# A recommendation tower on one core: turns moved one lookup sooner, table halves split by ScalarE's rounding, dots in uneven parts, last bias on TensorE

## The reference: what is computed

```python
e = jnp.stack([tbl_0[ids[:, 0]], ..., tbl_25[ids[:, 25]]], axis=1)   # (2048, 26, 128)
T = jnp.concatenate([dense[:, None, :], e], axis=1)                  # (2048, 27, 128)
Z = jnp.einsum('bnd,bmd->bnm', T, T)
iu0, iu1 = jnp.triu_indices(27, k=1)
z = Z[:, iu0, iu1]                                                   # (2048, 351)
h = jnp.concatenate([z, r_dense], axis=1)
h = jnp.maximum(h @ W_top1 + b_top1, 0.0)                            # 512 wide
h = jnp.maximum(h @ W_top2 + b_top2, 0.0)                            # 256 wide
y = h @ W_top3                                                       # (2048, 1)
```

## Time and profile before

| what | value |
|---|---|
| median of 3 runs | 508.34 us (504.71, 508.34, 509.56) |
| the profiled execution, its own time | 507.75 us |
| its span, first to last instruction | 505.9 us |
| mean granted clock of TensorE | 0.879 of full |
| busy: PE, weight load, DVE, ACT, POOL | 77%, 69%, 44%, 35%, 50% |

### The profile page before, as it was taken

How to read it: one execution, slowest core, us unless ns; L and a number is a source line. 1 busy time by engine, 2 the same in 40 slices (tenths; PEclk the granted TensorE clock), 3 DMA queues, 4 the chain that set the end, 5 groups by cost and what they waited for, 6 DMA issues and landing times.

```text
span 505.9 us, 9897 instructions
## 1 busy us (share of the span) xinstructions
PE 391.6 (77%) x4042; PEld 348.4 (69%) x4042; DVE 220.4 (44%) x786; ACT 174.9 (35%) x220; POOL 252.6 (50%) x263
## 2 busy tenths in 40 slices
PE   5841766695499858988599857988589866999997
PEld 3731656595398737978389745978379754988887
DVE  5521662584364404923346314734148223744322
ACT  4303540353225413343214422354114622244241
POOL 6776473647436554536544574456553575360000
PEclk9965796888689978988599987999699996999999
DMA  8961131125501322114311243113221151013221
GB/s 219 250 202 50 32 100 30 49 48 137 159 22 43 94 78 84 39 36 121 106 35 32 65 115 93 28 48 97 78 82 34 44 134 47 23 45 69 48 50 23
DMA packets 45878, 39.07 MB, mean 77 GB/s; under 512 B 32930, under 2 KB 39113, under 8 KB 45834
## 3 DMA queue, kind: packets, MB, share of 16 engines
q1 hardware_dynamic: 36014, 21.40, 16.0%
q0 software_dynamic: 8192, 16.79, 12.8%
q10 hardware_dynamic: 1628, 0.25, 0.3%
HBM read 32.40 MB, written 6.02 MB: 76 GB/s over the span
## 4 chain that ended last, share of the span: by engine, by line
PE 51%; another core or an unknown queue 28%; DVE 7%; issue 6%; ACT 6%; DMA 1%; DVEq 0%; SPq 0%; ACTq 0%
PE look_ps L756 25%; PE gram_ps L782 9%; PE mlp_ps L802 8%; DVE hot L467 5%; PE look_ps L766 5%; PE mlp_ps L812 3%; ACT T L618 2%; DVE gram L491 1%; ACT T L610 1%; ACT tab_hi L586 1%; PE look_ps L823 1%; PE look_ps L845 1%; DMA ids_all<-in_ids_dram 1%; DVE dense L480 0%
## 5 line engine op out<-in xcount | busy, mean ns | idle before, releaser
L421 POOL DMA_INDIRECT rows<-in_tbl_dram,ids_all x240 | 234.2, 976 | 196.6 <-PE look_ps L766 115.1
L467 DVE TENSOR_SCALAR hot<-ids_near 125x256 fp32r<-125x256 f16 x640 | 147.0, 301 | 151.0 <-remote 104.9
L756 PE MATMUL look_ps<-hot,tab_hi 125*128 125x256 f32 x616 | 162.4, 300 | 43.1 <-issue 32.5
L756 PE MATMUL look_ps<-hot,tab_lo 125*128 125x256 f32 x616 | 158.0, 293 | 5.7 <-issue 5.6
L756 PEld LDWEIGHTS look_ps<-hot,tab_hi 125*128 125x128 f32 x616 | 123.4, 200 | 47.7 <-issue 35.7
L756 PEld LDWEIGHTS look_ps<-hot,tab_lo 125*128 125x128 f32 x616 | 124.0, 201 | 6.1 <-issue 6.0
L618 ACT COPY T<-look_ps 128x384 f32<-128x384 f32 (+1 forms) x80 | 83.6, 1075 | 120.6 <-PE look_ps L766 108.1
L782 PE MATMUL gram_ps<-T 128*54 128x54 f32 x2048 | 72.9, 225 | 33.9 <-issue 27.1
L782 PEld LDWEIGHTS gram_ps<-T 128*54 128x54 f32 x2048 | 64.7, 140 | 45.1 <-issue 35.4
L610 ACT COPY T<-look_ps 128x512 f32<-128x512 f32 x32 | 38.6, 1206 | 108.0 <-PE look_ps L756 55.8
L491 DVE COPY gram<-gram_ps 128x432 f32<-128x432 f32 x64 | 38.0, 607 | 79.2 <-remote 53.4
(11 more groups left out here) (72 smaller groups left out, 146.0 us busy)
## 6 DMA issues: line engine op xcount, KB each, us to landing
dots<-gram SPq DMA_DIRECT2D x28, 182.2 KB
ids_near<-ids_rows SPq DMA_DIRECT2D x7, 640.0 KB
rows<-in_tbl_dram,ids_all POOLq DMA_INDIRECT x240
T<-in_tbl_dram SPq DMA_DIRECT2D x5, 448.0 KB
pairs<-dots SPq DMA_DIRECT2D x14, 117.0 KB
rows<-in_r_dense_dram SPq DMA_DIRECT2D x16, 64.0 KB
gram<-in_tbl_dram SPq DMA_DIRECT2D x2, 448.0 KB
pairs<-dots SPq DMA_DIRECT2D x7, 104.0 KB
```

The lines of the kernel that those rows point to most:

```text
L421: pool.indirect_dma_start(rows[:, t % 2, place[n], :], None, tables[n - 1], bass.IndirectOffsetOnAxis(ap=index[:, n - 1:n].bitcast(U32), a ...
L467: eq = nc.vector.tensor_scalar(hot[:VP, at % 2, c], ids_near[:VP, u % 2, k], float(c), None, ALU.is_equal)
L756: mm = pe.matmul(dst, w[:VP, k, c], hot[:VP, slot, c], start=(c == 0 and half == 0), stop=(c == CH - 1 and half == 1))
```

## The change

The change has six parts.

1. **Split of the tables.** `tab_hi` is now what ScalarE's write rounds the raw table to; `lead`, `top` and the semaphore `top_ready` are gone. ScalarE's copies for the first five tables stand ahead of the first look_out, those of the tables 1, 3 and 5 are moved from the loop to the start, and DVE subtracts in four instructions of 256 numbers in place of one of 1024 (`split`). Five raw buffers take the place of three, and the raw loads are issued sooner, ahead of the small weights.
2. **Turns.** In the first half of a unit u > 0, turn(u,1,2) stands ahead of look(u+1,1), turn(u,1,3) ahead of look(u+1,2), and turn(u,1,4) between the halves of layer1, on TensorE and on ScalarE alike. Unit 0 keeps its order.
3. **DVE in unit 0.** The splits of tables 1, 3 and 5 stand at other places, in one piece each.
4. **Dots.** The parts of a tile are 6, 8, 9 and 9 pieces, and 9, 9, 9 and 5 for the last tile.
5. **Last bias.** For the last tile the bias of the second layer is put into PSUM by one matmul (identity times bias) ahead of layer1, and DVE's addition after the last matmul is gone.
6. **Small weights** are issued on SP after load_dense(0, 1), ahead of the pair weights.

```diff
         def first_half(u):
             if u > 0:
-                return [("turn", u, 1, 0), ("turn", u, 1, 1), ("look", u + 1, 0), ("look", u + 1, 1),
-                        ("turn", u, 1, 2), ("look", u + 1, 2), ("turn", u, 1, 3), ("turn", u, 1, 4)]
+                return [("turn", u, 1, 0), ("turn", u, 1, 1), ("look", u + 1, 0), ("turn", u, 1, 2),
+                        ("look", u + 1, 1), ("turn", u, 1, 3), ("look", u + 1, 2), ("turn", u, 1, 4)]
...
+        def pieces(u, l):
+            ends = [9, 18, 27, NI] if u == END and l == 1 else [6, 14, 23, NI]
+            return list(zip([0] + ends, ends))
...
             def split(k):
-                lead(k)
-                rest(k)
+                dve.wait_ge(hi_ready, hi_count(k))
+                if k in WHOLE:
+                    dve.wait_ge(hot_looked, look_count(0, k))
+                for c in range(0, CH, 2):
+                    minus = nc.vector.tensor_tensor(tab_lo[:VP, k, c:c + 2], raw[k][:VP, c:c + 2],
+                                                    tab_hi[:VP, k, c:c + 2].bitcast(F32), ALU.subtract)
+                minus.then_inc(lo_ready, 1)
...
             def hi_out(k):
-                i = split_count(k) - 1
-                act.wait_ge(top_ready, i + 1)
-                nc.scalar.copy(tab_hi[:VP, k], top[2 if k in WHOLE else i % 2][:VP]).then_inc(hi_ready, 1)
+                act.wait_ge(raw_landed[k], 32)
+                nc.scalar.copy(tab_hi[:VP, k], raw[k][:VP]).then_inc(hi_ready, 1)
...
-            hi_out(0)
+            for k in LEADING[:5]:
+                hi_out(k)
             look_out(0, 0)
-            hi_out(2)
...
                 look(u + 1, 0)
+                turn(u, 1, 2)
+                look(u + 1, 1)
+                turn(u, 1, 3)
                 if u > 0:
-                    look(u + 1, 1)
-                    turn(u, 1, 2)
                     look(u + 1, 2)
                     layer1(u - 1, 0, 8)
-                    turn(u, 1, 3)
-                    layer1(u - 1, 8, 12)
                     turn(u, 1, 4)
-                    layer1(u - 1, 12, 16)
+                    layer1(u - 1, 8, 16)
...
+            pe.matmul(last_l2(1), ident[:], bias2[:], start=True, stop=False)
             last_layer1(1)
             last_layer2(1)
```

More of the change, by code:

```diff
@@ L17 @@
 MAX_ROUND = 4
-LOW_BITS = 12
 BLOCKS = 4
@@ L147, in dlrm_tower @@
         gram_flat = gram[:].rearrange("p s n q -> p (s n q)")
-        raw_slots = [table_at(spare, 0), table_at(spare, CH * D), table_at(gram_flat, 2 * CH * D)]
+        raw_slots = [table_at(spare, i * CH * D) for i in range(2)] + [table_at(gram_flat, i * CH * D) for i in range(3)]
         whole_raw = [table_at(w1[:].rearrange("p c f -> p (c f)"), 0), table_at(pairs[:].rearrange("p a c q -> p (a c q)"), 0),
@@ L303, in load_raw @@
             def load_raw(k):
-                if k not in WHOLE and in_turn.index(k) >= 3:
-                    sp.wait_ge(lo_ready, in_turn.index(k) - 2)
+                if k not in WHOLE and in_turn.index(k) >= len(raw_slots):
+                    sp.wait_ge(lo_ready, in_turn.index(k) - len(raw_slots) + 1)
                 src = tables[onehot[k]].rearrange("(p c) d -> p c d", c=CH)
@@ L362, in _ @@
             sp.dma_start(ids_all[:], ids_v).then_inc(ids_landed, 16)
-            for k in range(6):
+            for k in range(8):
                 load_raw(k)
             load_dense(0, 0)
-            load_raw(6)
-            load_small_weights()
-            load_raw(7)
+            load_raw(8)
             sp.wait_ge(ids_t_ready, UNITS)
@@ L484, in gram_out @@
                 if u == 0 and l == 0:
[L485 removed]
+                    dve.wait_ge(lo_ready, len(in_turn))
                 if u > 0 and l == 0:
                     dve.wait_ge(dots_stored, STORED * u)
[L488 removed]
+                for b, (first, end) in enumerate(pieces(u, l)):
                     dve.wait_ge(gram_done, BLOCKS * (2 * u + l) + b + 1)
[L490 to L493 removed]
+                    nc.vector.tensor_copy(gram[:, :, :, l * NI + first:l * NI + end],
+                                          gram_ps[:, b % 2, 0:2 * (end - first) * NV]
+                                          .rearrange("p (i s n) -> p s n i", s=2, n=NV)).then_inc(gram_free, 1)
             def y_out(u):
@@ L778, in products @@
                 src = T_tile(u, l).rearrange("p (g i s) n -> p g i (s n)", g=2, s=2)
-                for i in range(b * PER, (b + 1) * PER):
+                first, end = pieces(u, l)[b]
+                for i in range(first, end):
                     for g in range(2):
-                        at = (i - b * PER) * 2 * NV
+                        at = (i - first) * 2 * NV
                         mm = pe.matmul(gram_ps[64 * g:64 * g + 2 * NV, b % 2, at:at + 2 * NV], src[:, g, i],
@@ L845, in last_layer2 @@
                     mm = pe.matmul(last_l2(l), h1[:, c, l * P:(l + 1) * P], w2[:, c],
-                                   start=(c == 0), stop=(c == F1C - 1))
+                                   start=(c == 0 and l == 0), stop=(c == F1C - 1))
                 mm.then_inc(l2_done, 1)
```

93 lines of the change are left out of this document (29 added, 64 removed).

## The result

The changed kernel takes 532.51 us (median of 6 runs, 531.31 to 535.28) beside 508.33 for the kernel before: ratio 1.049, 95% interval 1.046 to 1.053. Timed once more (`after_again`) it took 532.06 beside 508.17, ratio 1.050 (1.045 to 1.054). The profiled execution has a span of 531.7 us.

A forecast was written before the change was run, and what follows sets the result against it. It took TensorE as busiest, but idling some 9 us a unit as its signals come late in long gather runs. 507.75 + 22.8 (turns) + 0.5 (split) = 531, given as 530; 8-in-10 range 491 to 538.

The forecast's parts named there:

- case A: Whole kernel: the long run of gathers in first halves makes TensorE's signals late; 530 us, 519 to 538; chance 0.56.
- the turns: First halves of units 1 to 6: earlier turns make a run of 8 gathers; 3.8 us more each, 22.8 in all.
- the split: Table split at the start: nothing gained up to 54.8 us, then split(9) waits for ScalarE's copy; +0.5 us, -1.8 to +1.1.
- The second half: Second halves of the units: order and run of 14 gathers stay, each moves as a whole; no cost.
- Uneven dots: Dots in uneven parts, each of 16 tiles: nothing, -0.2 to +0.2 us a tile.
- last bias: End of the kernel: DVE's 0.43 us addition goes, TensorE gains 0.45 us; zero, -0.5 to +0.5.
- Case B: First halves: turn 2 signals after GpSimd is free, so gathers run as 4 and 7; 495 us; chance 0.22.
- Case C: First halves: long runs do no harm, the dots gain 2.7 us in each of six; 492 us; chance 0.10.

The follow-up runs named there:

- turns_alone: The kernel before with only the new order of the turns in units 1 to 6; 528.51 us, ratio 1.037.
- broken: The changed kernel with GpSimd waiting for lookups before rounds 2 and 3 in first halves from unit 1 on; 501.42 us, ratio 0.986.
- turns_back: The changed kernel with the old order of the turns put back in units 1 to 6; 515.97 us, ratio 1.010.
- second: As `broken`, with GpSimd also waiting before rounds 2 and 3 in second halves; 358.97 us beside 362.88 on a fast chip, ratio 0.990.

## Why the prediction was right, point by point

The forecast, case A, was 530 us, and 532.5 came. The sum was 22.8 for the turns and 0.5 for the split; measured in the profile are 18.7 for the first halves, 4.2 for the second ones and 3.2 at the start, less 0.3 at the end. The mechanism and the place of the main term were right. That the total came within 2.5 us is partly luck: the main term was 4.1 too high, and two others that were put at 0 and 0.5 were 4.2 and 2.7 too low. In the second profile the same four are 15.1, 3.3, 0.7 and -0.2.

- *The turns make a run of 8, and it holds TensorE's signals.* Right in its place and its size: the run stands in all six units, DVE waits 5.3 us (5.9 in unit 0, from which it was taken), the half takes 30.0 us on the mean instead of the 30.6 forecast, the dots 3.43 (forecast 3.5). The clock is 0.50 for 4.35 us behind the run and 0.89 over the half. The term was 3.8 a half and is 3.1 (2.5 in the second profile). `turns_alone` and `broken` show it from both sides.
- *The second half keeps its run and costs nothing.* Missed by 4.2 us: each is 0.8 longer. In part it goes with the turns: `turns_alone` has 4.5 us more in its five second halves (2.5 of it in the one behind the broken run), `broken` 0.2. But `turns_back` still has 2.3, most of it in one half, so this is not settled. In unit 4 TensorE is busy 24.60 us there instead of 22.30, with 230 and 231 matmuls, at a clock of 0.79 instead of 0.84; it is the same work at a lower clock.
- *The table split, +0.5 (-1.8 to +1.1).* Missed in the profile, where the start is 3.2 us longer, and within the bounds in the second one of the same kernel, with 0.7; `broken` and `turns_back`, with the same start, have 3.6 and 3.9. The step that failed is that all up to 54.8 us would stay. DVE had waited 4.4, 9.5 and 13.8 us there, at 25.97, 39.13 and 54.83; its waits are now

```profile
35.35 1.71 DVE L456 TENSOR_SCALAR hot<-ids_near 125x256 fp32r<-125x256 f16 x8 [14.33 <-remote]
...
66.31 1.84 DVE L456 TENSOR_SCALAR hot<-ids_near 125x256 fp32r<-125x256 f16 x8 [14.88 <-remote]
```

  ended 3.7 and 3.5 us behind a run of gathers (23 up to 31.7, 16 from 40.3 to 62.8). At the first wait a signal came some 19 us late: the lookups of look(0, 0) were through at 16.0, and DVE and ScalarE go on at 35.3. In the kernel before the same signal reached ScalarE at 17.85. ScalarE's copies of the ids for the later units stand behind it, so they come at 36.2 instead of 19.8, and GpSimd has to wait for the ids (8.6 us, until 40.3). So the first run ends earlier, and the whole stage was cut anew. By these traces the start moves by how the runs of gathers fall, between 0.7 and 3.9 us for the same code, and not by what the edit of DVE's work saves. The detail did hold that split(9) waits for ScalarE's copy (1.32 us at 69.47).
- *Uneven dots and last bias: nothing.* Right for the end, which differs by 0.3 us: TensorE's two matmuls cost 0.43 us, and DVE's addition is gone. For the uneven dots in the units it was not tested alone; `turns_back`, which has them, takes 1.4 us more in its six first halves and 2.3 more in its five second ones.
- *Case B, the run breaks.* It was given 24.6 us for such a half, and the one unit in which it happened took 25.7; made to happen in all six, it gave 24.9 and 501 us. Its 495 was 6 us too low against `broken`: by the traces the first halves gain 12.6 us (13.2 were put), but the start costs 3.6 instead of 0.5, and the median of the four runs is 2.7 above the profiled one. That the following half can give some back, as in `turns_alone`, it left out as well.
- *Case C, long runs do no harm.* Wrong for the chip that was to be forecast, and true on two others. It rested on the Trainium skill's page "SBUF — State Buffer", section "Who interferes with whom", that DMA never contends with a compute engine. The traces agree as far as the data go: with the same 16.79 MB through the same queue by plain loads the kernel takes 362.9 us, no more than on a chip where nothing is late. No rule there covers what was seen, that during GpSimd's indirect gathers signals and instructions of TensorE are held back, on one chip and not on two others.

## What to carry to other kernels

Before you move work so that one engine's pauses close, look at what else gets through in those pauses: here a wait of GpSimd that looked idle (3.9 us) let signals through, and closing it cost 3 us in each first half. Where an earlier stage already has the order that an edit brings, price the edit by that stage. A pause made by waiting for the signal that must get through worked here, and a blind one of 1.2 us did not; longer blind ones were not tried where it matters. And time a kernel on more than one chip before you tune to a wait marked "remote": the waits that were tuned around here do not exist on two other chips.

## What the runs showed of the hardware

- The kernel before takes 508 us on one chip (11; the number of the first result's chip is not on record, but the time is the same there) and 363 on two others (15 and 10). On the slow one TensorE's signals come late during indirect gathers: 4.8 us in a run of 8 (335.5 to 340.3), 5.4 us in the run of 8 of the earlier trace rows (91.6 to 97.0), and 19 us in the run of 23 at the start of the changed kernel (16.0 to 35.3). From 5 to 15 us into a run its instructions start only 0.7, 1.4 or 2.1 us apart, in the dots a handful at a time. Both end 1 to 3.7 us behind the run. Gathers last 0.95 us and start every 1.25 us on the slow chip and on the fast ones. What differs between the chips no view of the profile shows, and I did not find it; whether it lies in the chip or in what else went on there at the time was not tested.
- On a slow chip the trace also lacks most records of signals: of the 4,096 by which the gathers report their landing it holds 1,189 (before), on a fast one 3,978 (`second`); with plain loads on the slow chip it holds all 4,096. So "remote" as a releaser probably means, for the most part, a signal whose record was lost. Longest sums of DVE's waits: 138.6 us "remote" in the changed kernel, none in `second`.
- The changed kernel itself was not timed on a fast chip. By `second`, whose waits cost GpSimd 1.8 us in all there, it should be about 1% faster than the kernel before: an estimate, not a measurement.
